# Another order of the 2,338 items of a twelve-stage decoder kernel

## The chip, the cores and the metric

One NeuronCore of one Trainium2 chip runs the whole program in a single launch. The metric is the device time of one execution in microseconds (us), the median of several runs. The chip's engines are called as in the profile: PE (TensorE matmuls), PEld (its weight loads), DVE (VectorE), ACT (ScalarE), POOL (GpSimd) and SP (SyncE, whose queue issues every DMA here, "SPq").

## The reference, cut to what is computed

The input `x` is (4, 512, 128): 4 batches of 512 tokens, model width 128. A context of 154 tokens per batch serves the cross attentions. Twelve stages follow each other, each as `x = layernorm(x + stage(x))`:

```python
CHAIN = ["L0a", "L0x", "ffn0", "heads1", "L1x", "moe1", "L2a", "L2x", "ffn2", "self3", "L3x", "moe3"]
# L0a, L2a: causal attention, 16 heads of width 8, rotated q and k
# L0x, L1x, L2x, L3x: cross attention to the context, 16 heads of width 8
# ffn0: quantised feed-forward with a depthwise convolution; heads1: attention among the heads of a token
# moe1: top 2 of 16 experts (with a capacity); moe3: 8 experts, dense; ffn2: gated feed-forward; self3: one-head attention
```

The 4 batches are independent, save for a running count of moe1's experts. So up to four chains of work can be interleaved.

## The kernel before

**Items.** The work is cut into items `(kind, stage and batch, number)`. `stage_items` (L150) lists them with what each needs. The six attention stages times 4 batches are the 24 *fronts*, numbered 0 to 23 in the order of `FRONT_ORDER` (0 to 3 are L0a, 4 to 7 L0x, 8 and 9 L1x, 10 L2a, 11 L1x, 12 L2a, 13 L1x, 14 and 15 L2x, 16 and 17 L2a, 18 and 19 L2x, 20 to 23 L3x). The other six stages are side stages. An item takes PE, and often DVE, ACT or POOL behind it, about 0.4 to 4 us.

**A front.** Its items come in this order:

- `project` (PE L782, L787): products for q, k, v. DVE copies them (L1244, L1248).
- `pieces` (POOL, `split_operands`, L1881): q, then k, are split into three bf16 pieces each, HQ and HK.
- `send` (SP, `load_operands`, L2000): the pieces are written to a DRAM scratch (L2010, L2014) and read back in another layout into QH and KH (L2025; L2032 and the `in_zrow` copy for a mask). Nothing of this takes PE.
- `max` (PE L824 and masks L830, then DVE L1261): scores q by k, of which DVE takes the negated row maxima. Two `max` items, one per half of the heads, make a step. A cross attention has 11 steps, a causal one 22. The first step of a front waits until its operands have landed (L801).
- `split`, `turn` (DVE, PE L840, ACT, DMA QH<-MT), then `pair` (PE L858, ACT's exponent L1683) and `value` (PE L897), `copy`, `out`, `mix`, and the tail `wo`, `square`, `mean`, `x`, which gives the stage's layernormed output to the next stage.

Side items that are named below: `gu` and `dn` are an expert's gate/up (PE L1017, L1018) and down product (PE L1024); `ew` is its weight load on SP's queue.

**What sets the order.** A list of words, `STEPS` (L257), says kind by kind which item comes next; a name with `*3` means three of it, and each `max` stands for a step of two. `ordered_items` (L337) takes the next waiting item of that kind, in the order of three short lists of stages and batches. `check_plan` (L455) asserts that every need stands ahead of its user. The result, PLAN, is walked once by each engine's program: every engine issues its own part of each item in this order, and waits in place for the semaphores that the item needs. The order is therefore the same on all engines, and an engine that waits for one item does none of the later ones. Products land in 3 single PSUM banks used in turn (`NRING` L606) and in two double ones for `pair`, `gu`, `g2`, `h0`, `s3`.

```python
                if F == 0:                                              # L797 to L801, PE ahead of a front's first max
                    pe.wait_ge(sem("fixed_rows"), 16 * 18)
                    ...
                pe.wait_ge(sem(f"operands_loaded{F % 3}"), operands_total(F))
```

Ahead of front 0's first max PE also waits for `halves_swapped` (L799): two copies CS<-const (`swap_halves`, L1984), which SP issues at the item `base`, once DVE has made `const` (DVE's part of `base`, L1169, its cast L1173). SP's part of `send` for front 0 is followed by `load_rest` (L1961): seven loads, among them pack<-in_pack of 2,284.5 KB.

Of the kernel before, what the change touches and what calls it, by code (L numbers as in the profile page):

```python
# [257 lines left out]
project*5 base pieces project send project*4 max*5 pieces max*9 send max*8 split project*2 max turn max project max pair  # L258
max project pair max pair max pair*2 max pair project value*3 pieces rest max pair*2 max pair max pair max value pair
max pair*2 max value max pair send pair max value max value pair max value copy pair*2 max value max project max value  # L260
max value pair max split pair project pair*2 max value turn pair max pair value max value*2 max pair*2 max value pair
copy max pair out pair out project max value max pair*2 max pair project max value max mix project pieces max value max
pair*2 max wo pair max value square pair max value max mean pair max value*2 max value pair copy max pair send x pair
max value max pair*2 value split out pair max pair turn pair*2 max value max value pair max pair value*2 max pair*2
value max pair value copy max pair*2 max value max pair*2 max value max project*2 out pair max value max pair*2 max
value max pair*2 masks value project mix project pieces pair*2 max value pair max value*2 pair max wo copy pair max
value send pair max pair value pair max pair value square max split pair*2 mean out x value turn value max pair project
value max pair*2 max value*2 pair max pair project*3 copy pair max pair value pieces max out value max pair*2 value max
pair mix pair max pair value*2 pair max value*2 pair max split pair wo send pair max value copy pair*2 max value max
pair square pair turn value max pair value max pair mean pair max value pair max value pair max value*2 max x pair value  # L270
pair max copy project out project pair max out project*2 pair value*2 pieces pair mix pair value pair send w0 copy split
wo turn out pair max value square pair max pair mean max value x max value project copy project out project*2 max mix
pair max wo max pair*2 max value square max mean max pair x pair max value pieces split send pair q0x pair value copy
pair*2 max q0t pair max h0 turn max h0 value*3 copy pair max silu0*3 out value silu0 out pair max h0t*2 mix pair h0b
pair max h0t wo h0b h0t square mean h0b*2 pair max x wo pair*2 q0x square value max pair*2 value q0t pair copy max h0
mean h0 value out silu0 value*2 silu0 copy max out silu0*2 h0t mix h0t h0b h0t h0b h0t h0b wo x h0b square wo max split
qkv mean qkv hs turn hv hs hm pair*2 qkv square value pair*2 hv value pair hs value hm qkv pair copy out pair mean
pair*2 tables2 pair value*2 hv hs hm value copy out mix x wo square mean hv hm x ht q0x wo q0t x square h0 mean x h0
# [1945 lines left out]
```

## Time and profile before

| what | us |
|---|---|
| median of 3 runs | 1750.06 |
| the 3 runs | 1750.06, 1750.02, 1759.99 |
| the profiled execution | 1757.96 |
| its span, first to last instruction | 1756.2 |
| PE busy in the span | 1378.9 |
| DVE busy | 1085.2 |
| ACT busy | 738.3 |
| POOL busy | 369.8 |
| mean granted clock of PE, share of 2.4 GHz | 0.866 |

The span and its 1.8 us of surroundings make the profiled execution's own time, which lies 7.9 us above the median, near the slowest of the three runs. An engine's busy time counts only what it computes; the rest of the span it waits, or issues. PEclk in a window is TensorE's granted clock as a share of 2.4 GHz: 0.50 is 1.2 GHz throughout.

### The profile page before, as it was taken

The page shows a single profiled execution, that of the slowest core. Times are in us where ns is not written, and L with a number is a line of the kernel's source. Part 1 is how long each engine was busy: PE and PEld are TensorE (multiplying, and loading weights), DVE is VectorE, ACT ScalarE, POOL GpSimd, SP SyncE. Part 2 cuts the span into 40 slices and gives each one's busy share as a digit, 9 for nine tenths or more (in the row PEclk, how much of TensorE's full clock was granted, in tenths as well). Part 3 has the DMA queues.
Part 4 walks back from the last instruction along what each step waited for, and adds up shares of the span by engine and source line. Part 5 has one row for each costly group of instructions (what it writes and reads, how often), then busy time and mean ns, then how long its engine had stood idle before and what let it go on. Part 6 is the DMA issues. An engine that isn't in the chain of part 4 may idle for free.

```text
span 1756.2 us, 25812 instructions
## 1 busy us (share of the span) xinstructions
PE 1378.9 (79%) x9530; PEld 656.8 (37%) x9530; DVE 1085.2 (62%) x2336; ACT 738.3 (42%) x1036; POOL 369.8 (21%) x475
## 2 busy tenths in 40 slices
PE   3568887785665686687577987988998999978986
PEld 1234332331331351343133544543344444434443
DVE  3648866778569579578766646756234524256766
ACT  1055654644323213214345542346644545532652
POOL 3034432006105206304432012022211100020000
PEclk8579988886567796798698989999999999988999
DMA  7421232100100310330222124131211321023011
GB/s 169 113 56 33 55 52 42 34 1 26 36 0 2 72 37 2 85 75 4 57 47 59 38 55 83 33 96 27 62 36 37 82 52 61 2 58 64 25 37 60
DMA packets 50072, 86.35 MB, mean 49 GB/s; under 512 B 13718, under 2 KB 42198, under 8 KB 45526
## 3 DMA queue, kind: packets, MB, share of 16 engines
q1 hardware_dynamic: 49950, 84.71, 21.0%
q8 instruction: 78, 1.28, 0.3%
q14 instruction: 44, 0.36, 0.1%
HBM read 66.95 MB, written 15.60 MB: 47 GB/s over the span
## 4 chain that ended last, share of the span: by engine, by line
PE 46%; DVE 18%; DMA 11%; POOL 7%; SPq 7%; issue 6%; ACT 5%; POOLq 0%; ACTq 0%; DVEq 0%
PE ps L897 5%; PE ps L1051 5%; PE ps L824 5%; DMA KH<-scratch 5%; DVE MX L1261 5%; PE ps L1017 4%; SPq L2025 4%; PE ps L1018 4%; PE ps L1024 3%; POOL SIDE L1937 3%; PE ps L830 3%; DMA scratch<-HQ 2%; PE ps L858 2%; PE ps L735 2%; ACT WORK L1683 2%
## 5 line engine op out<-in xcount | busy, mean ns | idle before, releaser
L1261 DVE TENSOR_REDUCE MX<-ps 128x3 f32<-128x462 f32 (+5 forms) x704 | 411.7, 626 | 233.4 <-PE ps L830 170.2
L1683 ACT ACTIVATE WORK<-ps 128x1024 f32<-128x1024 f32 (+1 forms) x352 | 319.7, 945 | 204.0 <-PE ps L858 123.9
L824 PE MATMUL ps<-KH,QH 48*128 48x154 bf16 (+5 forms) x1536 | 147.1, 279 | 178.0 <-DVE MX L1261 66.1
L824 PEld LDWEIGHTS ps<-KH,QH 48*128 48x128 bf16 (+1 forms) x1536 | 61.9, 99 | 334.7 <-DVE MX L1261 151.7
L897 PE MATMUL ps<-WORK,VA 128*18 128x512 f32 (+3 forms) x1536 | 171.4, 535 | 10.3 <-POOL WORK L1923 6.4
L1937 POOL TENSOR_TENSOR SIDE<-SIDE 128x512 f32<-128x512 f32 x64 | 113.1, 1799 | 269.1 <-ACT SIDE L1752 228.2
L1923 POOL TENSOR_SCALAR_AFFINE_SELECT WORK<-WORK 128x256 f32<-128x256 f32 (+1 forms) x192 | 93.8, 495 | 355.6 <-ACT WORK L1683 354.8
L1777 ACT ACTIVATE SIDE<-ps 128x512 f32<-128x512 f32 x96 | 57.3, 597 | 253.9 <-PE ps L1018 253.6
L858 PE MATMUL ps<-QH,KH 54*128 54x512 bf16 (+3 forms) x768 | 120.2, 359 | 13.8 <-ACT WORK L1683 10.8
L1507 DVE TENSOR_TENSOR SIDE<-SIDE,ps 128x512 f32<-128x512 f32 x96 | 65.6, 686 | 98.0 <-ACT SIDE L1777 97.5
L1024 PE MATMUL ps<-SIDE 128*128 128x128 f32 x768 | 111.0, 292 | 15.3 <-DVE SIDE L1507 13.0
L1017 PE MATMUL ps<-XT,SIDE 128*128 128x512 f32 x192 | 112.1, 668 | 6.8 <-DMA SIDE<-in_experts 6.7
L1024 PEld LDWEIGHTS ps<-SIDE 128*128 128x128 f32 x768 | 98.9, 200 | 42.9 <-issue 32.9
L1518 DVE SCALAR_TENSOR_TENSOR SIDE<-ps,SIDE 128x128 f32<-128x128 f32 x352 | 98.9, 343 | 18.6 <-PE ps L1024 16.7
L1018 PE MATMUL ps<-XT,SIDE 128*128 128x512 f32 x192 | 102.8, 618 | 0.0
L1876 POOL CAST HQ<-WORK 128x512 bf16<-128x512 f32 x23 | 14.2, 617 | 411.9 <-DVE WORK L1248 282.7
L858 PEld LDWEIGHTS ps<-QH,KH 54*128 54x128 bf16 x768 | 34.5, 99 | 100.8 <-issue 49.5
L946 PE MATMUL ps<-SQ,pack 128*128 128x512 f32 x96 | 61.1, 723 | 14.0 <-ACT SQ L1705 13.1
L735 PE MATMUL ps<-pack,SIDE 128*128 128x128 f32 x260 | 49.8, 337 | 28.2 <-DVE SIDE L1384 13.7
L782 PE MATMUL ps<-XT,pack 128*128 128x512 f32 x96 | 57.8, 711 | 14.2 <-DMA XT<-in_xT 10.1
L1626 ACT ACT_TABLE_LOAD x38 | 48.8, 1283 | 42.3 <-PE ps L858 13.3
L1316 DVE TENSOR_TENSOR XT<-YC,RS 128x512 f32<-128x512 f32 x48 | 36.2, 753 | 39.2 <-ACT RS L1715 39.1
(279 smaller groups left out, 2194.9 us busy)
## 6 DMA issues: line engine op xcount, KB each, us to landing
SIDE<-in_experts SPq DMA_DIRECT2D x96, 192.0 KB, 2.4
scratch<-HQ SPq DMA_DIRECT2D x48, 192.0 KB, 3.0
QH<-scratch SPq DMA_DIRECT2D x48, 192.0 KB
SIDE<-in_wide SPq DMA_DIRECT2D x8, 1024.0 KB, 6.6
QH<-scratch SPq DMA_DIRECT2D x48, 128.0 KB
scratch<-HK SPq DMA_DIRECT2D x16, 192.0 KB, 2.9
QH<-scratch SPq DMA_DIRECT2D x48, 64.0 KB
KH<-scratch SPq DMA_DIRECT2D x16, 192.0 KB
```

What stands on the lines that cost most here:

```text
L824: mms[b] = pe.matmul(banks[b][:, c * pitch:c * pitch + width], qr[b][:, h, t * 128:t * 128 + 128], kr[b][:, h, 0:width], start=(c == 0), s ...
L858: mm = pe.matmul(bank[:, b, q0 * (len(hs) == 1) + i * (S - q0):][:, 0:S - q0], kr[b][:, h, kt * 128:kt * 128 + 128], qr[b][:, h, q0:S], st ...
L897: mm = pe.matmul(ps[32 * j:32 * j + 2 * NV, UB, q0:S], lhsT.rearrange("p a c -> p (a c)"), PB[:, (PAIR_BASE[F] + where[pi]) % NSLOT, b, at ...
L1017: pe.matmul(banks[:, 0, :], gates(key, i)[:, 0:128], XT[:, b, :], start=True, stop=True)
L1018: pe.matmul(banks[:, 1, :], gates(key, i)[:, 128:256], XT[:, b, :], start=True, stop=True).then_inc(all_wide, 1)
L1024: mm = pe.matmul(bank[:, t * 128:t * 128 + 128], HID[n % 2][:, t * 128:t * 128 + 128], gates(key, i)[:, 256:384], start=True, stop=True, s ...
L1051: mm = pe.matmul(bank, hidden(l, k, c), src[:, k, :], start=(k == 0), stop=(k == FC - 1))
L1261: dve.tensor_reduce(MX[:, 32 * b + i0:32 * b + i0 + cnt], src, AX.X, ALU.max, negate=True).then_inc(freed, 1)
L1518: ins = dve.scalar_tensor_tensor(out=o, in0=p, scalar=s, in1=o, op0=ALU.mult, op1=ALU.add)
L1683: act.activation(PB[:, N % NSLOT, :, lo:hi], wide_banks("pair", F, n)[:, :, lo:hi], ACT.Exp).then_inc(sem("exp_done"), 1)
L1923: pool.affine_select(out=p, in_=p, pattern=pattern, compare_op=ALU.is_ge, fill=0.0, base=0, channel_multiplier=-1).then_inc(sem("selected" ...
L1937: pool.tensor_tensor(out[:, hs], SC1[i][:, hs].unsqueeze(2).broadcast_to([128, n_heads, DH, H]), v.broadcast_to([128, n_heads, DH, H]), AL ...
```

## The change

`STEPS` is replaced as a whole. Nothing else differs: the same 2,338 items, the same three lists of stages and batches, the same instructions, buffers and waits for each item. Two lines of the table, before and after (the others are of the same sort):

```diff
-project*5 base pieces project send project*4 max*5 pieces max*9 send max*8 split project*2 max turn max project max pair
+project*5 pieces project*5 send base max*2 pieces max*2 project max*4 project max*2 project max*3 project send max*2
```

Two places show what the words do. The first is the start of SP's queue, around front 0's `send` and the item `base` (CS<-const is `base`'s, scratch and QH/KH<-scratch are `send`'s, CT to mconst are `load_rest`). Before, in a piece of the difference:

```order
 L1982 DMA XT<-in_xT 128x1536
-L1988 DMA CS<-const 64x1088 x2
 L2010 DMA scratch<-HQ 64x3x512 x2
 L2014 DMA scratch<-HK 64x3x512 x2
```

and in the kernel after, further down:

```order
L2025 DMA KH<-scratch 8x4096 x2
L1963 DMA CT<-in_cT 128x640
L1964 DMA pack<-in_pack 128x4569
L1965 DMA SIDE<-in_mask_q 128x640
L1966 DMA SIDE<-in_mask_k 128x512
L1967 DMA SIDE<-in_mask_k 32x512
L1968 DMA SIDE<-in_mask_c 128x640
L1969 DMA mconst<-in_mconst 3x1
L1988 DMA CS<-const 64x1088 x2
L2010 DMA scratch<-HQ 64x3x512 x2
```

The two CS copies, which stood ahead of front 0's transfers, now stand behind them and behind the seven loads.

The second place is PE ahead of front 9's first max (L1x, batch 1; L779 is its last projection, L824 with 154 columns its first max step; L1017, L1018 and L1024 are experts of moe1, batch 0). Before:

```order
698 L779 MATMUL ps<-pack,CT 32x128 x4
699 L1017 MATMUL ps<-XT,SIDE 128x512
700 L1018 MATMUL ps<-XT,SIDE 128x512
701 L1024 MATMUL ps<-SIDE 128x128 x8
702 L1017 MATMUL ps<-XT,SIDE 128x512
703 L1018 MATMUL ps<-XT,SIDE 128x512
704 L824 MATMUL ps<-KH,QH 128x154 x6
```

After:

```order
704 L1024 MATMUL ps<-SIDE 128x128 x8
705 L1017 MATMUL ps<-XT,SIDE 128x512
706 L1018 MATMUL ps<-XT,SIDE 128x512
707 L1024 MATMUL ps<-SIDE 128x128 x4
708 L1017 MATMUL ps<-XT,SIDE 128x512
709 L1018 MATMUL ps<-XT,SIDE 128x512
710 L1017 MATMUL ps<-XT,SIDE 128x512
711 L1018 MATMUL ps<-XT,SIDE 128x512
712 L1024 MATMUL ps<-SIDE 128x128 x8
713 L1017 MATMUL ps<-XT,SIDE 128x512
714 L1018 MATMUL ps<-XT,SIDE 128x512
715 L824 MATMUL ps<-KH,QH 128x154 x6
```

Between the last projection and the first max step PE has two `gu` and two `dn` (four products each) before, and four `gu` and five `dn` after. Counted from the k projection, which stands earlier, it is 4 `gu` and 4 `dn` before and 6 `gu` and 5 `dn` after.

## Rows read from the trace of the kernel before

**Rows 1.** The page: span, busy time by engine, chain by engine
```profile
span 1756.2 us, 25812 instructions
...
PE 1378.9 (79%) x9530; PEld 656.8 (37%) x9530; DVE 1085.2 (62%) x2336; ACT 738.3 (42%) x1036; POOL 369.8 (21%) x475
...
PE 46%; DVE 18%; DMA 11%; POOL 7%; SPq 7%; issue 6%; ACT 5%; POOLq 0%; ACTq 0%; DVEq 0%
```

**Rows 2.** Waits of PE: line waited for: us, times, longest
```profile
PE ps L824 <- DVE MX L1261: 66.1, 100, 4.8
PE ps L824 <- DMA KH<-scratch: 62.6, 12, 11.5
PE ps L824 <- DMA KH<-in_zrow: 20.4, 3, 8.7
PE ps L824 <- DMA KH<-MK: 17.3, 3, 7.4
```

**Rows 3.** Timeline, front 15: start us, us, engine line op [idle before]
```profile
1023.30 0.61 POOL L1876 CAST HQ<-WORK 128x512 bf16<-128x512 f32 x1 [46.82 <-DVE WORK L1248]
...
1028.47 0.49 POOL L1879 TENSOR_TENSOR HK<-WORK,HK 128x160 bf16<-128x160 f32 x1
...
1028.99 1.24 SPq L2014 DMA_DIRECT2D scratch<-HK  x2
...
1032.98 2.25 SPq L2025 DMA_DIRECT2D KH<-scratch  x6
...
1041.93 0.57 PE L824 MATMUL ps<-KH,QH 48*128 48x154 bf16 x6 [6.53 <-DMA KH<-scratch]
```

**Rows 4.** Windows, k projection to first max, of fronts 6, 7, 9, 15
```profile
core 0: us, PE busy (x) PEld busy (x) DVE busy (x) ACT busy (x) POOL busy (x), PEclk, DMA share, GB/s
...
271.70:291.00 19.30, 10.75 (x79) 4.16 (x78) 11.44 (x35) 8.40 (x11) 5.15 (x8) 0.89 0.47 84
300.80:319.40 18.60, 12.57 (x122) 4.59 (x122) 14.87 (x39) 11.54 (x15) 5.13 (x8) 0.95 0.45 85
...
592.80:614.40 21.60, 11.97 (x58) 6.98 (x58) 8.67 (x27) 2.57 (x5) 6.74 (x11) 0.92 0.60 118
...
1022.50:1041.90 19.40, 11.72 (x77) 4.82 (x76) 5.93 (x15) 8.80 (x12) 5.14 (x8) 0.89 0.60 111
```

**Rows 5.** Groups by line, whole span
```profile
L1017 PE MATMUL ps<-XT,SIDE 128*128 128x512 f32 x192 | 112.1, 668 | 6.8 <-DMA SIDE<-in_experts 6.7
L1024 PE MATMUL ps<-SIDE 128*128 128x128 f32 x768 | 111.0, 292 | 15.3 <-DVE SIDE L1507 13.0 <-DVE SIDE L1518 1.1 <-DVE MX L1261 0.5
L1018 PE MATMUL ps<-XT,SIDE 128*128 128x512 f32 x192 | 102.8, 618 | 0.0
```

**Rows 6.** Timeline of SP's queue, 24 to 58 us
```profile
24.61 1.18 SPq L1988 DMA_DIRECT2D CS<-const  x2
...
36.50 0.44 SPq L1964 DMA_DIRECT2D pack<-in_pack  x1
...
39.63 1.24 SPq L2010 DMA_DIRECT2D scratch<-HQ  x2
...
54.89 2.30 SPq L2025 DMA_DIRECT2D QH<-scratch  x6
```

**Rows 7.** Windows, first to last max, fronts 0, 8, 9; sum of 24
```profile
47.40:83.50 36.10, 19.39 (x193) 10.79 (x193) 24.91 (x42) 0.00 (x0) 0.00 (x0) 0.50 0.46 118
...
478.90:527.50 48.60, 33.18 (x130) 16.54 (x130) 31.65 (x72) 11.40 (x17) 0.00 (x0) 0.66 0.00 0
614.40:656.10 41.70, 37.18 (x196) 21.95 (x196) 30.29 (x75) 5.97 (x10) 0.00 (x0) 0.92 0.14 39
...
sum 974.20, PE 836.03 PEld 413.22 DVE 670.63 ACT 420.50 POOL 185.20; mean PE 34.83 PEld 17.22 DVE 27.94 ACT 17.52 POOL 7.72
```

**Rows 8.** Windows behind five waits: the first (front 9), the sum
```profile
614.40:621.20 6.80, 6.79 (x25) 4.02 (x26) 3.40 (x8) 0.00 (x0) 0.00 (x0) 0.50 0.09 29
...
sum 37.30, PE 35.51 PEld 19.41 DVE 20.89 ACT 7.21 POOL 0.00; mean PE 7.10 PEld 3.88 DVE 4.18 ACT 1.44 POOL 0.00
```

More of the change, by code:

```diff
@@ L257 @@
 STEPS = """
-project*5 base pieces project send project*4 max*5 pieces max*9 send max*8 split project*2 max turn max project max pair
[L259 to L277, printed above, removed]
@@ new lines @@
+value qkv value hm copy pair*2 hs pair hv hm value hv qkv pair mean hs value out hm pair x value hv copy out mix wo hm
+square x mean ht q0x wo q0t x square h0 mean x h0 project silu0*4 project h0t*2 h0b h0t h0b h0t h0b project*2 h0b pieces
+send wo max q0x max*2 q0t max*2 h0 max h0 square silu0 max silu0*3 max h0t*2 h0b h0t h0b h0t h0b max h0b max wo max qkv
+mean split qkv hs turn pair*2 hv pair hs hm qkv hv pair*3 value hs value hm square hv qkv value pair*3 copy value*2 pair
+value hs hm out mean copy out x hv mix wo hm square mean x*2 ht log top ew*2 wo gu square ew rank gu mean dn x dn ew gu
@@ new lines @@
+ew project gu dn*2 project ew project gu*2 project dn pieces dn ew*2 gu dn ew send gu*2 ew dn*2 ew gu ew max gu max dn*2
+ew max gu max gu dn*2 ew max ew gu max dn max ew gu max gu max dn*2 max acc max split qkv*2 hs wo square turn hv hs pair
+qkv pair*2 hm hv value*2 pair*2 mean qkv value pair hs pair copy x pair hm pair hv project pair hs value hm project
+value*2 project copy out*2 mix project wo hv project square mean hm x ht log top ew wo gu pieces square ew*2 rank gu
+mean dn send ew dn x ew gu project*2 gu max dn project ew dn max ew gu max gu dn ew max dn max gu max ew gu max dn*2 max
@@ new lines @@
+square pair max mean max value x max project max pair project max*2 pair max out pair max project*2 max mix out max
+pieces value max pair wo square max value max copy send mean split out turn mix x max wo project square pair*2 max mean
+pair max x pair value max pair log pair max pair value project ew max top pair ew pair value pair value project*2 pieces
+pair*2 max value pair max ew pair value pair max gu*2 rank value*2 copy max pair value dn send pair*2 out ew dn pair*2
+max value*2 split pair*2 max ew gu*2 turn max pair value pair dn value ew max pair dn gu*2 ew value max pair dn*2 ew
@@ new lines @@
+pair max gu ew gu value*2 max copy pair dn out dn gu max ew value*2 mix dn gu ew gu max pair dn wo pair dn ew max ew
+pair square pair ew value pair max pair mean max x gu copy project gu dn value dn gu ew project split value*2 ew dn turn
+gu*2 copy dn out dn project pair*2 acc out wo project mix value square pieces send wo mean square max pair x mean max
+pair*2 x max pair log project top max ew*2 gu value rank project gu dn project*2 dn ew*2 gu ew gu dn project ew dn max
+gu*2 dn max value dn pieces ew*3 gu copy max send pair*2 max dn gu max gu dn pair max pair max split dn ew gu ew value
@@ new lines @@
+hid2 max pair*2 max wo max pair value max pair*2 max pair value max value max wide copy pair*2 value max pair value max
+out g2*2 square value copy max g2 max g2 wide out mean x split hid2 mix hid2*3 wo hid2*2 turn square hid2*2 pair*2 wo
+pair*2 f3 mean s3 square x s3 fk3 value pt3*4 mean x wo value f3 square mean s3 x s3 project pair project fk3 pt3*4 pair
+wo square value copy log project ew project pair top ew*2 pair out mean gu*2 pieces send max dn*2 x max gu ew max
+project*2 dn max gu max pair value ew max dn pair max ew gu project max gu value project max value pieces send max ew
@@ L329 @@
+ew gu*2 dn ew dn gu ew dn gu square gu dn*2 fin mean acc wo square x mean x fin*2
 """.split()
```

95 lines of the change are left out of this document (44 added, 51 removed).

## The prediction

> **What bounds the kernel now.** I read the page first. PE is busy 1378.9 of 1756.2 us, DVE 1085.2; no engine is full, and the chain that ended last runs 11% over DMAs and 7% over SP's queue [rows 1]. So look for where PE stands still for a transfer. PE's waits say it: 66.1 us in 100 small waits for DVE's maxima, and 100.3 us (62.6 + 20.4 + 17.3) in only 18 waits at L824 for KH [rows 2]. L824 is the score product of a `max` item, and KH is what `send` fetches, so these 18 are waits of a front's first max step.
>
> The timeline of front 15 shows one of them whole [rows 3]. Its k projection ends at 1022.5, POOL splits q and k from 1023.3 to 1029.0, the scratch writes and the read-back are issued up to 1035.2, and PE starts at 1041.9, after 6.5 us of nothing. Set against that the work that PE had in the meantime: in the 19.4 us from the k projection to the first max it was busy 11.7 [rows 4]. Fronts 6, 7 and 9 read the same: 19.3, 18.6 and 21.6 us, filled with 10.8, 12.6 and 12.0 us [rows 4]. The latency of a cross front is thus about 19 us, that of a rotated causal one some 5 us more (POOL's longer split), and the order before puts too little work between.
>
> **The change, step by step.** The same instructions run, so I price places only.
>
> *1. Waits for the first max.* For each front I added up PE's time for the items between its last q/k projection and its first max, in both orders, each item at the time that its own instructions took in the trace. Front 9 as the example: 4 `gu` and 4 `dn` before, 6 and 5 after. A `gu` is (112.1 + 102.8)/96 = 2.24 us, a `dn` 111.0/96 = 1.16 [rows 5], so 2 x 2.24 + 1.16 = 5.6 us more. But SP's queue counts too: front 9's `send` stands behind an `ew` that waits for a `dn`, and from that `dn` to the first max the work grows only by 4.1 us. Of its wait (7.4 us, the longest of the MK row [rows 2]) 3.3 are left. In the same way: fronts 4, 5, 6 and 7 gain 2.6, 7.4, 8.4 and 10.2 us of cover against waits of 1.1, 4.7, 3.1 and 3.7, so nothing is left; 8, 17 and 19 gain 5 to 7 against 4.8, 6.3 and 4.5, nothing left; 10, 12, 13, 15 and 16 keep 2.1, 2.2, 1.8, 0.7 and 0.3; front 14 keeps 4.6 (its cover is counted from the last causal select ahead of `pieces` on POOL); front 18 gains none and keeps 1.8; front 22 gains 3.9 against 11.5 and keeps 7.6. The 89 us of these fronts (100.3 less front 0's 10.9, from 36.5 to 47.4) fall to 25, a gain of 64. Some of the moved items were timed at the low clock and will be shorter, so I take 58. Bounds: 79 if every one goes that gains cover at all, 45 if the items shrink by a third.
>
> *2. Front 0 starts later.* `base` now stands behind `send` on SP. Before, SP issued the two CS copies at 24.6 [rows 6], and PE started at 47.4 on its operands. Now they are issued behind `load_rest`, at about 39.6, where the next write stood, and PE waits for them. What a transfer issued there meets is in the trace: the query write of front 1, issued at 39.63 behind the 2,284.5 KB of pack (36.50), was not there for SP's next step until 54.89 [rows 6]. So the CS copies land near 55 and PE starts some 8 us later: +8. Bounds: 0, if small copies get past the load, and 12. The page "DMA: Bandwidth & Descriptors" of the Trainium skill, in its section on latency, names about 2 us as the fixed cost of a DMA; priced by that alone the copies would be there at 42, ahead of the operands, and the sum would be 8 us lower. The same page's section on queues says that each DMA engine takes descriptors in ring order, which is what the row shows.
>
> *3. Cover taken out of the max phases.* The work now ahead of the first max was elsewhere: mostly inside other max phases, where it ran while DVE reduced. Over the 24 phases PE is busy 836 us and DVE 671 in 974 [rows 7]; by the same item times the new order leaves PE 783 there, 53 us less. What bare steps look like is seen in front 0, with nothing between: 36.1 us for 24.9 of DVE and 19.4 of PE, 22 steps of 1.64 us [rows 7], in which both engines wait for each other by turns. I cut both orders into short stretches (3 to 30 items) and took the busier engine's time in each: the new order is longer by 1 to 7 us in sum. That is the low bound, since it knows no latencies. The high bound is that all 53 us stop being hidden. I take 14, near the low end, as most phases still have PE above DVE.
>
> *4. The clock.* Behind a long wait PE runs at half speed. After the waits of fronts 9, 10, 15, 16 and 17 the granted clock is 0.50 for 37.3 us in all, with PE busy 35.5 of them [rows 8]; at the full level that is half the time, 18 us. The other waits have such stretches too, but in phases where DVE also binds. I take -18, bounds 0 and -30.
>
> *5. Other distances* (turn to pair, log to rank, value to out, heads1's chain) I compared the same way: some shrink and some grow by 1 to 6 us, in sum about nothing. The loads of the experts and of ffn2 keep their places relative to their users within a few items.
>
> Sum: -58 + 8 + 14 - 18 = -54. Against the profiled execution's own 1757.96 that is 1704. It lies 7.9 above the median, and since the runs before show both 1750.0 and 1760.0 I take half of that off: **1700 us**. A measurement here tells about 1% (17 us) from no change.
>
> **The rivals.**
>
> *A. The max phases lose what the fronts gain.* One mechanism: the 53 us moved out of the phases were fully hidden there and now cost their full length, and the thinner phases fall to the low clock, so the 18 us do not come. For it: front 8's phase, where PE (33.2) only matches DVE (31.7), took 48.6 us at a clock of 0.66, and front 0's ran at 0.50 throughout [rows 7]. Against it: front 9's phase, with PE above DVE, lost only 4.5 us to gaps [rows 7]. Price: -58 + 8 + 53 + 0, and some 15 us more for phases 1, 8 and 9 at half clock: +18, so 1776, and **1772** as a median. It decides from 50 us of lost cover on. The Trainium skill has the rule in "TensorE: Matmul & The Clock Gate", in the section on a second failure mode (depth-cycling of PSUM): short idles between groups of matmuls, often enough, make the clock oscillate. Front 0's phase agrees ((36.1 - 19.4)/22 = 0.76 us without PE in each step, clock 0.50).
>
> *B. Half of it.* The waits go, but what fills them runs faster than in the trace and what is late next (DVE's maxima, the exponent) takes half of the gain: -27, so 1731, **1728** as a median. For it: PE's waits for DVE's maxima are many and short, 66.1 us in 100 [rows 2], and the new order makes more of them. Against: late in the kernel PE is near full in most windows.
>
> *C. The change does not do what it says.* SP issues in order, so a `send` that stands behind an `ew` or a `turn` starts only when these may; if the landings move back with the max steps, the 18 waits stay and front 0's +8 is all: **1755**. For it: front 9, above. Against: for the other fronts the item ahead of `send` on SP's queue is ready before the split is done, in both orders.
>
> **How the numbers follow.** Forecast 0.75, B 0.11, A 0.07, C 0.07. The forecast's own range comes from its bounds, not all at one end at once: 1663 to 1728. Faster by over 1% (below 1732.6) is nearly all of the forecast's share and over half of B's: 0.81. Within 1%: C, the rest of B and a little of the forecast: 0.13. Slower by over 1%: most of A: 0.06. The range 1664 to 1742 leaves out A and C, some 0.14, and a little at the low end.
>
> **What would show it.** Right, if PE's waits for KH fall from 100 us to 30 to 45 in all, the longest two being front 0's (near 19 us) and front 22's (7 to 8); if PE's first max starts near 55 instead of 47.4; if the mean granted clock rises above 0.866; if DVE's maxima are waited for somewhat more than 66 us. Wrong in term 1, if fronts 5 to 8 and 15 to 17 still wait over 2 us each. Wrong in term 2, if the first max stays at 47. Wrong in term 3 (rival A), if the waits for KH are gone and the 24 max phases with less PE work are not shorter.

## The result and the profile after

The changed kernel takes 1689.2 us (median of 4 runs, 1681.2 to 1693.0) beside 1752.8 for the kernel before (the three runs above and a fourth, 1755.6): a ratio of 0.963, 95% interval [0.960, 0.966]. Four single executions among all the runs below, of 2,221 to 6,492 us and two of them of e4_max_late, were slow ones and are left out of every time and ratio. Forecast were 1700 us and 1664 to 1742. The profiled execution took 1692.3 us, 65.7 less than the one of before; the forecast worked out from it was 54 less.

The page of the kernel after: span, busy time by engine, granted clock in 40 slices, chain by engine (of before [rows 1]).

```profile
span 1690.6 us, 25807 instructions
...
PE 1359.3 (80%) x9530; PEld 648.6 (38%) x9530; DVE 1084.9 (64%) x2336; ACT 736.6 (44%) x1035; POOL 372.9 (22%) x475
...
PEclk8559899987666797799779999999999999989989
...
PE 54%; DVE 20%; DMA 7%; ACT 6%; issue 5%; POOL 4%; SPq 4%; ACTq 0%; DVEq 0%; POOLq 0%
```

DVE, ACT and POOL are busy as long as before. PE is busy 19.6 us less on the same products, because less of them falls at 1.2 GHz: summed from the clock records of the two traces, PE is busy 311.8 us at that level before and 267.4 after (mean clock 0.866 and 0.882; an estimate of the same work at the full level, with half of that time taken off, is 1223 us before and 1226 after). It stands still 46.0 us less (span less busy time: 377.3 before, 331.3 after). On the chain DMA fell from 11 to 7% and SP's queue from 7 to 4%.

PE's waits after: line waited for, us in total, times, longest (of before [rows 2]).

```profile
PE ps L824 <- DVE MX L1261: 63.2, 83, 4.0
PE ps L871 <- DMA QH<-MT: 21.1, 5, 9.6
PE ps L1017 <- DMA SIDE<-in_experts: 19.8, 5, 7.5
PE ps L858 <- ACT WORK L1683: 17.9, 18, 4.4
PE ps L824 <- DMA CS<-const: 17.9, 1, 17.9
PE ps L897 <- ACT WORK L1683: 16.9, 5, 8.8
...
PE ps L824 <- DMA KH<-scratch: 13.1, 4, 8.3
```

The 100.3 us for KH are 13.5 (13.1 here, 0.4 in another row), with front 22's the longest. Front 0 now waits 17.9 us for CS instead of 10.9 for KH. The wait for MX is not longer than before. New are three long waits for an expert's load.

The windows of the max phases of fronts 0, 8 and 9 and the sum of all 24 (of before [rows 7]); columns: us; busy time of PE, PEld, DVE, ACT, POOL; PEclk; DMA share; GB/s.

```profile
57.00:99.10 42.10, 29.02 (x209) 14.24 (x209) 27.64 (x46) 0.63 (x1) 9.57 (x10) 0.50 0.22 42
...
482.00:524.10 42.10, 25.71 (x121) 13.81 (x120) 31.03 (x71) 8.69 (x14) 0.00 (x0) 0.68 0.00 0
623.10:652.60 29.50, 24.25 (x149) 13.70 (x148) 23.97 (x57) 4.18 (x7) 0.00 (x0) 0.96 0.09 27
...
sum 913.50, PE 779.19 PEld 384.15 DVE 668.17 ACT 422.59 POOL 190.76; mean PE 32.47 PEld 16.01 DVE 27.84 ACT 17.61 POOL 7.95
```

The phases lost 56.8 us of PE's work and got 60.7 us shorter: PE stands still in them 134.3 us, against 138.2 before. Outside the phases the kernel takes as long as before (777 us, 782 before), with 37 us more of PE's work in it.

SP's queue from 36 to 60 us, where the CS copies now stand (of before [rows 6]).

```profile
36.39 0.43 SPq L1964 DMA_DIRECT2D pack<-in_pack  x1
...
39.31 1.16 SPq L1988 DMA_DIRECT2D CS<-const  x2
40.74 1.28 SPq L2010 DMA_DIRECT2D scratch<-HQ  x2
45.89 5.77 SPq L2014 DMA_DIRECT2D scratch<-HK  x2
57.64 2.28 SPq L2025 DMA_DIRECT2D QH<-scratch  x6
```

The copies are issued 2.9 us behind `pack`, and PE starts its first max 17.7 us after their issue, at 57.0. Before it was 47.4. The view of DMA issues from 24 to 62 us gives the time from issue to landing (last figure, median of the two copies), before and then after:

```profile
CS<-const SPq DMA_DIRECT2D x2, 136.0 KB, 5.1
```

```profile
CS<-const SPq DMA_DIRECT2D x2, 136.0 KB, 16.5
```

### The profile page after: what moved, and what is told of

It reads as the page before. It is cut to its first block, busy times and chain, and to the rows that moved or that the text cites. A ratio compares the mean times of both kernels' runs of the same rounds, so it can differ in the third digit from the quotient of the medians.

```text
span 1690.6 us, 25807 instructions
## 1 busy us (share of the span) xinstructions
PE 1359.3 (80%) x9530; PEld 648.6 (38%) x9530; DVE 1084.9 (64%) x2336; ACT 736.6 (44%) x1035; POOL 372.9 (22%) x475
## 4 chain that ended last, share of the span: by engine, by line
PE 54%; DVE 20%; DMA 7%; ACT 6%; issue 5%; POOL 4%; SPq 4%; ACTq 0%; DVEq 0%; POOLq 0%
PE ps L897 6%; PE ps L1051 6%; PE ps L824 6%; DVE MX L1261 5%; PE ps L1017 5%; PE ps L1024 4%; PE ps L1018 4%; POOL SIDE L1937 3%; PE ps L830 3%; PE ps L735 3%; PE ps L782 3%; PE ps L858 2%; DMA SIDE<-in_experts 2%; SPq L2025 2%; ACT WORK L1683 2%
## 5 line engine op out<-in xcount | busy, mean ns | idle before, releaser
L824 PE MATMUL ps<-KH,QH 48*128 48x154 bf16 (+5 forms) x1536 | 142.4, 271 | 104.5 <-DVE MX L1261 63.2
L897 PE MATMUL ps<-WORK,VA 128*18 128x512 f32 (+3 forms) x1536 | 165.7, 518 | 20.8 <-ACT WORK L1683 14.9
L824 PEld LDWEIGHTS ps<-KH,QH 48*128 48x128 bf16 (+1 forms) x1536 | 59.1, 96 | 268.2 <-DVE MX L1261 156.2
L858 PE MATMUL ps<-QH,KH 54*128 54x512 bf16 (+3 forms) x768 | 118.0, 352 | 19.8 <-ACT WORK L1683 17.9
L1017 PE MATMUL ps<-XT,SIDE 128*128 128x512 f32 x192 | 112.1, 668 | 20.1 <-DMA SIDE<-in_experts 19.8
L1024 PE MATMUL ps<-SIDE 128*128 128x128 f32 x768 | 110.1, 290 | 18.4 <-DVE SIDE L1507 14.9
L1024 PEld LDWEIGHTS ps<-SIDE 128*128 128x128 f32 x768 | 97.6, 198 | 49.4 <-issue 36.2
L1518 DVE SCALAR_TENSOR_TENSOR SIDE<-ps,SIDE 128x128 f32<-128x128 f32 x352 | 98.8, 343 | 18.5 <-PE ps L1024 16.5
L1018 PE MATMUL ps<-XT,SIDE 128*128 128x512 f32 x192 | 102.5, 616 | 0.0
L782 PE MATMUL ps<-XT,pack 128*128 128x512 f32 x96 | 66.0, 796 | 23.2 <-DMA XT<-in_xT 14.5
L858 PEld LDWEIGHTS ps<-QH,KH 54*128 54x128 bf16 x768 | 33.7, 97 | 98.4 <-ACT WORK L1683 54.7
L1626 ACT ACT_TABLE_LOAD x38 | 48.8, 1283 | 30.2 <-PE ps L858 7.6
L946 PE MATMUL ps<-SQ,pack 128*128 128x512 f32 x96 | 55.1, 657 | 7.7 <-ACT SQ L1705 7.3
L897 PEld LDWEIGHTS ps<-WORK,VA 128*18 128x18 f32 x1536 | 30.2, 98 | 75.8 <-issue 29.2
```

What stands on the lines that cost most here:

```text
L782: mm = pe.matmul(bank[:, 0:src.shape[1]], w, src, start=True, stop=True)
L824: mms[b] = pe.matmul(banks[b][:, c * pitch:c * pitch + width], qr[b][:, h, t * 128:t * 128 + 128], kr[b][:, h, 0:width], start=(c == 0), s ...
L858: mm = pe.matmul(bank[:, b, q0 * (len(hs) == 1) + i * (S - q0):][:, 0:S - q0], kr[b][:, h, kt * 128:kt * 128 + 128], qr[b][:, h, q0:S], st ...
L897: mm = pe.matmul(ps[32 * j:32 * j + 2 * NV, UB, q0:S], lhsT.rearrange("p a c -> p (a c)"), PB[:, (PAIR_BASE[F] + where[pi]) % NSLOT, b, at ...
L1017: pe.matmul(banks[:, 0, :], gates(key, i)[:, 0:128], XT[:, b, :], start=True, stop=True)
L1018: pe.matmul(banks[:, 1, :], gates(key, i)[:, 128:256], XT[:, b, :], start=True, stop=True).then_inc(all_wide, 1)
```

## The experiments

Each is a new `STEPS`, with the same items and instructions, so nothing is left out of the computation. A cover is PE's work, in us of the trace, between a front's last q/k projection and its first max. The table puts all of them side by side. They ran in four groups, in each of which the kernel before was timed too (medians 1752.3, 1750.5 and 1750.0, and 1747.9 for the last; 1.000 and the 1750.1 of the table are the three runs above); between groups the ratios compare better than the times. Time and ratio are of the timed runs, the rest of the one profiled execution: PE busy (the page), PE still (span less busy), and PE's waits in groups, each summed from the rows of the view of PE's waits. "KH, CS" are the first max steps, "MX" is L824 waiting for maxima, "turn" is L840's wait for MP and every wait for QH<-MT (split, turn, first pair), "experts" is L1017's for in_experts. The five groups add up to 10 to 13 us less than "PE still": that rest no row of the view names.

| kernel | time | ratio to before, 95% | PE busy | PE still | KH, CS | MX | turn | experts | all other |
|---|---|---|---|---|---|---|---|---|---|
| before | 1750.1 | 1 | 1378.9 | 377.3 | 100.3 | 66.1 | 24.0 | 6.7 | 170.0 |
| e0_after | 1687.0 | 0.965 [0.962, 0.969] | 1353.1 | 331.0 | 30.3 | 64.9 | 24.5 | 17.6 | 180.9 |
| e1_base_first | 1678.2 | 0.958 [0.954, 0.962] | 1356.0 | 323.8 | 23.8 | 64.7 | 25.6 | 21.5 | 175.6 |
| e7_best | 1678.5 | 0.959 [0.957, 0.961] | 1358.3 | 316.6 | 22.1 | 70.0 | 23.7 | 6.3 | 182.4 |
| e5_ew_first | 1699.2 | 0.971 [0.968, 0.975] | 1360.5 | 334.7 | 51.9 | 64.2 | 24.0 | 3.5 | 178.4 |
| e3_send_late | 1711.1 | 0.977 [0.973, 0.980] | 1359.5 | 349.7 | 34.3 | 64.8 | 20.9 | 35.5 | 181.5 |
| e6_bare17 | 1715.5 | 0.980 [0.978, 0.982] | 1368.8 | 339.8 | 30.9 | 80.0 | 22.5 | 19.4 | 175.1 |
| e8_max_early | 1751.8 | 1.001 [0.998, 1.004] | 1384.0 | 370.3 | 83.5 | 70.2 | 19.7 | 3.2 | 181.7 |
| e2_base_late | 1759.3 | 1.004 [1.001, 1.007] | 1381.1 | 381.7 | 101.5 | 65.0 | 24.7 | 6.2 | 173.5 |
| e10_max_late9 | 1758.4 | 1.003 [1.001, 1.006] | 1376.1 | 384.1 | 68.2 | 87.1 | 34.4 | 5.3 | 179.5 |
| e11_shift | 1754.0 | 1.003 [1.001, 1.005] | 1375.0 | 370.5 | 30.5 | 72.2 | 51.5 | 20.6 | 185.0 |
| e4_max_late | 1762.2 | 1.008 [1.005, 1.011] | 1387.6 | 371.3 | 30.2 | 91.9 | 33.7 | 24.5 | 181.1 |
| e9_late_even | 1788.6 | 1.020 [1.014, 1.026] | 1394.7 | 393.5 | 32.6 | 90.2 | 33.4 | 17.7 | 208.3 |

**e0_after**: the changed kernel as it is.

> The changed kernel again, as the mark for the others that are made from it. Expected 1689 us (0.963 of the kernel before, as measured), and in its trace the same pattern as in the first: PE's wait for CS<-const near 18 us, for KH some 13 us, for the expert loads (SIDE<-in_experts) some 20 us. A theory that puts one of these down to chance would see it change here.

The pattern repeats: CS 17.6, KH 12.7, experts 17.6. PE's busy time was 6.2 us less than in the first profile of the same kernel (254.0 us of it at 1.2 GHz, 267.4 there), so differences of that size between two profiles prove nothing.

**e1_base_first** and **e2_base_late**: the price of `base` behind `load_rest`, from both sides.

```diff
 e1_base_first, against the changed kernel
-project*5 pieces project*5 send base max*2 pieces max*2
+project*5 base pieces project*5 send max*2 pieces max*2
 e2_base_late, against the kernel before
-project*5 base pieces project send project*4 max*5
+project*5 pieces project send project*4 base max*5
```

> The changed kernel with `base` ahead of front 0's pieces and send, as it stood before. Theory (the two CS copies are late only because they are issued behind load_rest): the first max starts at 47.5 us again instead of 57.0, PE's wait for CS<-const (17.9 us) is replaced by one of some 11 us for KH, and the time falls by 8 to 10 us against the changed kernel. Rival (the start is paid back later, since front 1's items are not ready sooner): the first max starts 9 us earlier but the phase of front 0 or the wait for front 1 grows by as much, and the time stays within 3 us.

> The kernel before with `base` moved to directly ahead of front 0's first max, so that its CS copies stand behind load_rest as in the changed kernel, and nothing else. Theory: the first max starts at 55 to 57 us instead of 47.4 and the whole kernel gets 8 to 10 us slower. Rival (the delay is absorbed later, as front 1 waits for DMAs anyway): 0 to 3 us slower.

PE's first max in e1_base_first, then in e2_base_late, from the timelines (start, us, what; in brackets the idle time before and what ended it):

```profile
48.03 0.61 PE L824 MATMUL ps<-KH,QH 48*128 48x512 bf16 x2 [11.34 <-DMA KH<-scratch]
```

```profile
57.39 0.61 PE L824 MATMUL ps<-KH,QH 48*128 48x512 bf16 x2 [17.53 <-DMA CS<-const]
```

The one item moves the start by 8 to 10 us in both kernels, and the wait changes its name with it. In the changed kernel undoing it is worth 8.8 us (1687.0 to 1678.2), as expected. In the kernel before it costs 7 us (0.4%, interval 2 to 12 us), which decides neither for the 8 to 10 expected nor against the rival's 3. Its trace shows something of both: the first max of a front stands 9 to 14 us later than before up to front 15 and 5 to 7 us later from front 16 on, so part of the delay is taken up by waits on the way (the KH waits of fronts 5, 14, 15 and 16 are each 1.3 to 1.8 us shorter).

The copies themselves land 5.5 us after their issue in e1_base_first and 16.4 us in e2_base_late, by the same view as above. In either kernel it is some 5 us when they are issued ahead of the load and some 16 behind it.

**e5_ew_first**: three loads of experts (not four, as its expectation says) ahead of the sends. One of the three edits, at front 9:

```diff
-ew*2 gu dn ew send gu*2 ew dn*2 ew gu ew max
+ew*2 gu dn ew*2 send gu*2 dn*2 ew gu ew max
```

> The changed kernel with four loads of experts issued ahead of a front's send instead of behind it: those of moe1 batch 0 expert 9 (ahead of front 9's send), batch 1 expert 3 (front 10's), batch 3 expert 9 (front 16's, with the down product whose space it reuses). Theory (an expert's load waits behind the read-backs on SP's in-order queue): PE's waits for SIDE<-in_experts, 19.8 us in three places, fall to 2 us or less, and the time falls by 10 to 18 us. Rival (the queue only passes the delay on: the sends now wait for the loads): the first max of fronts 9, 10 and 16 waits 2 to 6 us each instead, and the time stays within 4 us.

The expert waits fall to 3.5 us (to 2 or less was expected), and the kernel gets 12 us slower: the rival's mechanism, and worse than its price. SP's queue around front 10's `send` in the changed kernel (e0_after), then here:

```profile
708.80 1.28 SPq L2051 DMA_DIRECT2D SIDE<-in_experts  x3
710.19 1.29 SPq L2010 DMA_DIRECT2D scratch<-HQ  x2
```

```profile
709.59 12.53 SPq L2051 DMA_DIRECT2D SIDE<-in_experts  x4
722.23 1.29 SPq L2010 DMA_DIRECT2D scratch<-HQ  x2
...
728.50 2.25 SPq L2025 DMA_DIRECT2D KH<-scratch  x6
```

The group of loads stretches over 12.5 us instead of 1.3. Expert 3 goes into the space of expert 0, so its load waits for expert 0's down product, and the `send` behind it waits too: it starts 12 us later. Front 10's first max then waits 12.9 us instead of 0, front 9's 6.8, front 16's 3.4.

**e3_send_late**: meant to place `pieces` and `send` later. It did not do so, and its expectation describes it wrongly.

```diff
-ew wo gu pieces square ew*2 rank gu mean dn send ew dn x ew gu project*2 gu max
+ew wo gu pieces send square ew*2 rank gu mean dn ew dn x ew gu project*2 gu max
```

> The changed kernel with `pieces` and `send` of thirteen fronts (4 to 10, 12, 13, 15, 16, 17, 19) placed later, so that PE has as much work between the split and the first max as in the kernel before (within about 2 us); PE's own order stays that of the changed kernel. Theory (this distance is what the change wins by): the waits for KH of these fronts come back, 68 us in the kernel before, with the low clock behind them: 60 to 85 us slower than the changed kernel, that is 1745 to 1770. Rival (the gain lies in the rest of the order, and the waits went because everything ahead of them moved): under 25 us slower.

I had set the work between `send` and first max to what stands between projection and first max in the kernel before. In the changed kernel `send` stands nearer to the first max than that in twelve of the thirteen fronts, so there it moved earlier, as the edit at front 10 shows; only front 5's moved later (19.6 us of PE's work behind it, now 14.1). So this run says nothing for or against the distance. It says two other things. Front 5, the one that moved later, waits 3.9 us for KH instead of 0. And where a `send` moved ahead of expert loads (fronts 9, 10 and 16), the loads wait behind it. SP's queue at front 10, then PE behind it:

```profile
717.97 1.28 SPq L2010 DMA_DIRECT2D scratch<-HQ  x2
...
726.15 2.25 SPq L2025 DMA_DIRECT2D KH<-scratch  x6
728.45 0.83 SPq L2051 DMA_DIRECT2D SIDE<-in_experts  x2
```

```profile
738.07 2.05 PE L1017 MATMUL ps<-XT,SIDE 128*128 128x512 f32 x2 [11.95 <-DMA SIDE<-in_experts]
```

PE could have had expert 1 at 726.1; its load is issued at 728.45, behind twelve read-back pieces, and PE starts at 738.1. Three such waits (11.95, 10.4 and 10.0 us) make most of the 35.5 of the table. The kernel lost 20 to 24 us by ratio and times; between the traces it is 25.1, of which 18.7 are PE standing still. Together with e5: neither place of an expert's load beside a `send` is free.

**e8_max_early**: the distance taken out of the changed kernel (front 9 here).

```diff
-ew send gu*2 ew dn*2 ew gu ew max gu max dn*2
+ew send max gu*2 max ew dn*2 max ew gu ew gu dn*2
```

> The reverse of e4_max_late on the changed kernel: the first 1 to 4 max steps of thirteen fronts (4 to 10, 12, 13, 15, 16, 17, 19) are drawn forward, so that 56 us of PE's work leave the stretches between the q/k projections and the first max and stand in the max phases again. e3_send_late did not do this: POOL and SP run ahead of PE, so a later place in PE's list did not delay a split or a send. Theory (distance on PE between projection and first max is worth its waits): waits of 35 to 50 us for KH come back in fronts 5, 7, 8, 9, 10, 19, and with the low clock behind them the kernel gets 35 to 60 us slower than the changed kernel (1722 to 1747). Rival (what e4_max_late showed: cover in front of the first max and cover inside the phases are worth the same): KH waits come back, but MX and expert waits fall by nearly as much, under 15 us slower.

(Its sentence on e3_send_late is wrong, as said above.) The whole gain is gone: 1751.8 us, as the kernel before and 62 to 65 us above the changed one (by the ratios, by the times), more than the expected 35 to 60. Between the two profiles, 70 us apart, 39.3 us are PE standing still and 30.9 are PE busy longer on the same work, at a clock of 0.861 instead of 0.886 (busy at 1.2 GHz for 322.4 us instead of 254.0). PE's waits at L824 here:

```profile
PE ps L824 <- DVE MX L1261: 70.2, 78, 4.5
PE ps L824 <- DMA KH<-scratch: 38.8, 10, 7.8
...
PE ps L824 <- DMA CS<-const: 17.6, 1, 17.6
PE ps L824 <- DMA KH<-MK: 16.2, 3, 10.0
```

KH came back with 53 us. The work that went back into the phases saved nothing there: MX is 70.2 against 64.9, and PE's idle time in the 24 phases 148 us against 138. Only the expert waits fell, from 17.6 to 3.2, since PE comes later to the gate/up products. The rival is out: in the changed kernel the whole gain hangs on where the first steps of these thirteen phases stand.

**e4_max_late**: the same distance given to the kernel before (front 9 here).

```diff
-gu pieces dn*2 send ew gu max dn max ew gu ew gu dn*2 max gu ew gu
+gu pieces dn*2 send ew gu dn ew gu ew gu max dn max dn max gu ew gu
```

> The kernel before with nothing changed but the place of the first 1 to 6 max steps of fourteen fronts (4 to 10, 12, 13, 15, 16, 17, 19, 22): they are postponed behind the work that followed them until PE has as much ahead of the first max as in the changed kernel. Theory (the cover ahead of the first max is worth its waits, and the max phases lose little by it): these fronts' 80 us of waits fall to 15 to 25, the mean clock rises to 0.875 or more, the time falls by 50 to 75 us. Rival A (the phases lose what the fronts gain): the waits fall as much, but PE's waits for MX and its idle time inside the 24 phases grow by 50 us, and the time falls by less than 15 us.

The waits for KH fall by 70 us (without front 0 from 89.4 to 20.0; the changed kernel has 12.7), and the time does not fall: it is 0.8% longer than before (13 us; 2.7 between the profiled executions, of which the one of before was among the slower of its kernel). In the time this is what rival A forecast, in the trace only a part of it: summed over the 24 phases, from the first L824 of each to its last, PE's idle time grew from 137.8 to 158.6 us, where the expectation has 50 more, so most of what came back stands outside the phases. Four of the rows that moved:

```profile
PE ps L824 <- DVE MX L1261: 91.9, 128, 5.2
PE ps L1017 <- DMA SIDE<-in_experts: 24.5, 6, 9.8
PE ps L824 <- DMA KH<-scratch: 22.4, 5, 10.2
...
PE ps L858 <- DMA QH<-MT: 8.3, 3, 6.6
```

Against the kernel before, MX costs 26 us more, experts 18, turned maxima 10, the rest 11: 64 of 70 are back. And PE is busy 8.7 us longer, at 0.865, with 325.8 us of it at 1.2 GHz against 311.8 before: the long waits went and the clock did not rise. That splits what the prediction had tied together: the absence of the KH waits does not bring the clock's gain by itself. Three of the new expert waits show where a part of it went: behind each, PE's first products run at 1.2 GHz, as they did behind the KH waits (L1017 takes 2.04 us for two there, and 1.10 at 716.6 us, behind a wait of 0.5).

**e10_max_late9**: e4 in only the nine fronts without a moe1 load right behind their send (front 5 here).

```diff
-max value copy pair*2 max value max pair square pair turn value max pair value max pair mean pair
+value copy pair*2 value pair square pair turn value pair value pair mean max pair max*2 value max
```

> e4_max_late with only the nine fronts whose send has no load of a moe1 expert right behind it (4, 5, 6, 7, 8, 12, 17, 19, 22): 42 us of KH waits in the kernel before. If e4_max_late lost because the waits at fronts 9, 10, 13, 15, 16 only moved to the gate/up products (SIDE<-in_experts 24.5 us there against 6.7), this one keeps the gain of its own nine: expert waits near 7, KH waits near 65, time 15 to 25 us below before. If the phases lose what the fronts gain, the time stays within 8 us of the kernel before.

The expert waits stay away (5.3 us) and the gain too: KH falls by 32 us, MX rises by 21, the turned maxima by 10, all other by 10. So the experts alone were not what e4 lost by. MX carries most of it:

```profile
PE ps L824 <- DVE MX L1261: 87.1, 125, 5.2
```

**e9_late_even**: e4 with its steps spread evenly by PE's time (front 17 here).

```diff
-max pair max*2 value max*2 pair max value max*2 value pair max out pair*2
+max pair value max pair value max value max pair max out pair max pair value
```

> e4_max_late with the steps of its fourteen fronts spread evenly over the phase by PE's time, the first and the last step and all other items in place. Steps with nothing between them and the one before fall from 31 to 22 in these phases. If e4_max_late lost by bunching (a step without cover waits for DVE's maxima, and PE falls to the low clock), PE's waits for MX fall from 92 us to 75 or less, the clock rises and the time falls to 1740 or less. If the cover missing in the phases as a whole is what costs, it stays within 8 us of e4_max_late's 1765.

MX is 90.2, no better, and the kernel 21 us slower still (by the ratios). An even spread by PE's time did not help: front 8's phase alone grew from 44.6 to 55.0 us, and the all-other column by 27. That bunching is the cause was not shown here, nor excluded, since 22 bare steps (with no work of PE between them and the step before) remained in these phases, by the expectation's count.

**e11_shift**: the phases of e4 begun later and ended later, with few steps left bare (front 9 here).

```diff
-gu pieces dn*2 send ew gu max dn max ew gu ew gu dn*2 max gu ew gu
+gu pieces dn*2 send ew gu dn ew gu ew gu dn*2 max gu ew gu dn ew dn ew*2 max gu max gu
```

> The kernel before with the max phases of the same fourteen fronts (4 to 10, 12, 13, 15, 16, 17, 19, 22) begun 1 to 6 steps later, as in e4_max_late, but not made up for inside the phase: every step takes the place of a later one, the last ones stand behind the old end of the phase, one after each 0.6 us or more of PE's work, and split and turn follow them. PE's cover ahead of the first max is that of the changed kernel (within 3 us). Max steps with no PE work between them and the one before number 40 over all 24 phases in the kernel before, 32 in the changed one, 58 in e4_max_late, 34 here. Theory (the cover pays only if no step is left bare): KH waits near 31 us as in e4_max_late, MX waits back from 92 to 75 us or less, the clock above 0.87, and the time 30 to 60 us below the kernel before, 1690 to 1720. Rival (the phases' later end costs what their later start gains: split, turn and the first pair come later): MX waits fall as said, but PE waits 20 us or more longer for turned maxima, exponents and expert loads, and the time is within 10 us of the kernel before.

MX falls back to 72.2 us, as the theory said, which fits e4's rise of MX having come from the bare steps. The time does not follow (1754.0; the profiled execution lies 10.7 us below the one of before, the timed runs 0.3% above). The rival's sentence holds: what was paid at MX is now paid at turn and pair.

```profile
PE ps L824 <- DVE MX L1261: 72.2, 111, 5.4
PE ps L824 <- DMA KH<-scratch: 20.7, 4, 10.2
PE ps L1017 <- DMA SIDE<-in_experts: 20.6, 6, 8.2
PE ps L871 <- DMA QH<-MT: 19.7, 9, 8.9
PE ps L840 <- DVE MP L1276: 17.8, 9, 4.5
PE ps L858 <- DMA QH<-MT: 14.0, 5, 7.1
```

The last three rows are split, turn and first pair: 51.5 us, 24.0 before. One of them in the timeline of PE, front 16:

```profile
1172.06 1.05 PE L897 MATMUL ps<-WORK,VR 128*18 128x512 f32 x8
1180.26 0.61 PE L858 MATMUL ps<-QH,KH 54*128 54x512 bf16 x2 [7.15 <-DMA QH<-MT]
```

The phase ends later and its items are used up, so nothing is left to cover the way of the maxima through DVE, PE, ACT and a DMA into QH.

**e6_bare17**: one phase stripped.

```diff
-max pair value out pair max copy pair*2 max value max pair*2 out wide
+max*22 pair value out pair copy pair*2 value pair*2 out wide
```

> The changed kernel with one max phase stripped: the items that stand between the 22 steps of front 17 (27.4 us of PE's time in the trace) come behind the phase's last step but one. It measures the price of lost cover. In the changed kernel the phase takes 40.1 us, PE busy 38.1 and DVE 27.8. If all the moved work was hidden and now costs its length, the bare phase takes 36 us as front 0's did in the kernel before, at the low clock, and the kernel gets 27.4 + 36 - 40 = 23 us slower. If the phase only falls back to what DVE needs (25 us, at a clock kept high), it gets 12 us slower. If the moved items run faster elsewhere, less than 8 us.

Slower by 1.5% of the ratios, 26 us, and by 24.6 in the profiles. The windows of front 17's phase and of the stretch behind it, in the changed kernel (e0_after), then here:

```profile
1139.30:1179.40 40.10, 38.10 (x428) 16.75 (x427) 27.85 (x52) 29.43 (x36) 11.51 (x24) 1.00 0.08 27
```

```profile
1135.20:1170.10 34.90, 18.10 (x195) 10.44 (x194) 24.91 (x42) 0.69 (x1) 0.00 (x0) 0.58 0.08 30
1170.10:1205.00 34.90, 31.77 (x235) 10.04 (x232) 5.40 (x16) 28.10 (x34) 11.55 (x24) 0.88 0.00 1
```

The first line is the changed kernel, the second and third are this one. The bare phase takes 34.9 us with PE busy 18.1 at a clock of 0.58, much like front 0's bare phase before (36.1 us at 0.50) [rows 7]: without cover PE and DVE take turns. The 27.4 us taken out shorten the phase by 5.2 only, so cover in the middle of a phase is worth most of its length, in one phase at least. The first theory (23 us) was right.

**e7_best**: e1 with four more moves (front 22 here).

```diff
-gu*2 pieces send max dn*2 x max gu ew max project*2 dn
+gu*2 pieces send dn*2 x gu ew project*2 dn gu max*2
```

> A version meant to beat both: the changed kernel with `base` ahead of front 0's send (as in the run that tried it alone, 1678), the first max of front 22 behind 25.7 instead of 17.4 us of PE's work (four steps postponed) and of front 18 behind 21.6 instead of 17.9, and two gate/up items that waited for their expert's load (moe1 batch 1 expert 3, batch 3 expert 9) placed one to three items later. Expected: the KH waits of fronts 22 (7.5) and 18 (1.7) gone, the two waits for experts (2.8 and 5.8) down to 2 in all, so 12 to 15 us less than with `base` alone: 1664 to 1668. If the phases of 18 and 22 lose as much or the loads are then late at the next item, 1675 to 1680.

Both aims were met: front 22's first max waits for nothing, as its row in PE's timeline shows by naming no wait, and the expert waits are 6.3 us.

```profile
1501.91 0.37 PE L824 MATMUL ps<-KH,QH 48*128 48x154 bf16 x6
```

Yet the time is that of e1_base_first, 1678.5 beside 1678.2, though the profile shows 5 us less: MX took 5 us and the all-other column 7, and fronts 10, 16 and 15 wait 3.4, 3.3 and 3.2 us at their first max instead (front 15 waited 1.5 in e1_base_first). The sentence for the failing case (1675 to 1680) holds. e1 and e7 are the two versions that beat both kernels, by some 9 us or 0.5% against the changed one; which of the two is the faster can't be told.

## Why the prediction was right, and where it was not

The time was right (1689 in 1664 to 1742), and the mechanism that carried it was the one predicted: e8_max_early takes it out and loses everything. But the number is closer than its terms are: terms 1 and 3 were off by 18 and 14 us to one side, term 5 by 20 to the other, and that they cancelled is luck. Between the two profiles, as measured: fronts 1 to 23 at their first max -75.9, front 0 there +7.0, all other waits +20.5 (those inside the phases among them), standing still that no row names +2.4, PE's busy time -19.6: -65.6.

*Term 1, waits for the first max: -58 predicted.* Fronts 1 to 23 fell from 89.4 to 13.5 us, -76, inside the bounds of 45 to 79. Fronts 5 to 8, 16 and 17 wait for nothing and 15 for 1.3, as predicted. Fronts 22 (8.3; predicted 7.6), 18 (2.8; 1.8), 19 (0.7; nothing) and 12 (0.4; 2.2) keep something; 9, 10, 13 and 14 keep nothing, where 3.3, 2.1, 1.8 and 4.6 were predicted. For fronts 9 and 10 a reason is in the trace: PE waits 5.1 and 5.2 us just before them for an expert's load, and what it waits there it does not wait at the first max. Front 16, which came out as predicted, has the same behind it: 7.5 us for an expert's load up to 1064.9, and its first max at 1069.5. These three waits make 17.8 us, and with them set against it the term is -58, the number predicted. So the cover was right, and the sum over fronts missed that a wait can move to the item ahead of the first max. The same exchange is in e8 (KH up 53, experts down 14).

*Term 2, front 0 starts later: +8.* Shown: the start moved by 9.6 us. The wait is 17.9 us (near 19 was predicted), 7.0 more than before, and PE's wait for its input at the very start is 4.4 longer (14.5 us at L782 for in_xT, 10.1 before). `base` alone is worth 8.8 us in the changed kernel and some 7 in the one before.

*Term 3, cover taken out of the phases: +14.* Measured about nothing: PE's idle time in the phases went from 138.2 to 134.3, and MX, which was to rise somewhat, fell from 66.1 to 63.2. The step that failed was the low bound's: it held that thinner phases must cost at least a little. In the changed order they don't. Counted from the two orders, 27 steps have no item of PE between them and the step before, against 37 before (e11_shift's expectation, by a count of its own, has 32 and 40), although 57 us less of such work stand in the phases: it is spread better over them. That is a reading of the orders and not a proof. e11_shift supports it (32 such steps and an MX of 72 us, against 50 and 92 in e4), but the count is not all: e8_max_early has the same 27, with more cover in the phases, and its MX is 70.2.

*Term 4, the clock: -18.* PE's busy time fell by 19.6 us in the first profile and 25.8 in the second. The size was right, though part of it is the execution that was profiled: it read a clock of 0.866, and the executions of the kernel before read 0.863 to 0.880, 0.871 on average. The reason was too narrow. I had tied it to the low clock behind the KH waits. In e4_max_late those waits are gone and PE is busy 8.7 us longer. Over all the runs PE is busy longer where it stands still more, but only roughly: in the table 1353 to 1361 us of work go with 317 to 350 us of standing, 1375 to 1395 with 370 to 394. Taken run by run it does not hold: e6_bare17 stands still 10 us less than e3_send_late and is busy 9 longer, and e10_max_late9 stands 13 us more than e4_max_late and is busy 11 less. What moves with the busy time is how much of it falls at 1.2 GHz (254 us in e0_after, 270 in e3, 285 in e6, 303 in e10, 326 in e4). Which waits cause that no run separates.

*Term 5, other distances: about nothing.* This was the worst of the five. All waits but those for KH and CS grew from 266.8 to 287.3 us, +20.5. Experts are 13.1 of it, the exponents (L858 and L897 on WORK) 17.2, turned maxima 5.0 (QH<-MT), and others fell. The failing sentence was that the experts' loads "keep their places relative to their users within a few items". They did, within six; but on SP's queue three had moved up to the first place behind a `send` (from the fourth, second and third), and on PE their gate/up products had come to stand ahead of that front's first max instead of behind it. SP, then PE at expert 9 of moe1, batch 3, in the kernel after:

```profile
1049.97 2.25 SPq L2025 DMA_DIRECT2D KH<-scratch  x6
1052.26 0.61 SPq L2036 DMA_DIRECT2D KH<-in_zrow  x2
1052.91 1.05 SPq L2051 DMA_DIRECT2D SIDE<-in_experts  x2
```

```profile
1064.93 2.04 PE L1017 MATMUL ps<-XT,SIDE 128*128 128x512 f32 x2 [7.49 <-DMA SIDE<-in_experts]
```

The prediction read SP's queue for front 0 and front 9 and not for the loads behind the sends. For the exponents' 17.2 us no run shows the cause.

*The rivals.* C is out (its 1755 does not follow from its own words either: +8 on the profiled execution is 1766, 1762 as a median). B's mechanism did come, at a smaller price: waits of the kind it names took 20.5 of the 68.9 us back and not half, by the exponent, as it said, and the experts, but not by DVE's maxima. A had 7% and did not come in this change, yet its outcome is real: the same distance, given to the kernel before in three ways (e4, e10, e11), gained nothing. The waits move on to MX, to turn and pair, to the experts. So the distance is needed for the gain (e8) but does not bring it alone. An item-by-item sum, as in term 1, can't see where a wait moves: it would have given e4 its 50 to 75 us as well, and did, in its expectation. What in the rest of the changed order keeps those other waits at +20 us instead of +63 stays open. The bare steps are probably part of it (e11 against e4: MX 20 us less) but not all, and no run here adds the missing part to the kernel before. One reading that stood for A was too loose: front 0's phase shows a granted clock of 0.50 throughout, so its short idles go with a low clock, not with one that swings between the two levels.

## What to carry to other kernels

Work that fills a wait for a transfer may be missed where it stood: moving it cost nothing in the changed kernel and the whole gain in three other orders. Before counting such a gain, name what each moved item covered before, and look at the step that comes out of the other end of the phase (here split, turn and first pair), since postponing a start postpones that too. In a kernel whose every engine walks one list, an item's place matters against its neighbours on its own queue: list them for SP, above all bulk loads that carry a wait of their own, and read from each run both PE's idle time and its busy time, as in these runs both moved. An edit that is meant to move something later should be shown to do so, from the order itself, before its run is believed.

## What the runs showed of the hardware

- Two CS copies of 136 KB issued at 39.3 us, 2.9 us behind a bulk load of 2,284.5 KB, took 16.5 us from issue to landing, and PE started 17.7 us after their issue. Issued ahead of the load they took 5.1 to 5.5 us (before, e1_base_first). Copies that small were not passed ahead of the load. Two writes of HK behind it stretch over 5.77 us on SP's queue, where they take 1.24 for front 15 [rows 3]; the copies are not the reason, as these writes stretch over 5.36 us in the kernel before too.
- A bare phase kept TensorE low even in the second half of the kernel (e6_bare17): granted clock 0.58 with PE busy 18.1 of 34.9 us, where the covered phase had 1.00 with 38.1 of 40.1, and 0.88 in the 34.9 us behind it, with PE busy 31.8 of them.
- Removing 70 us of long waits did not raise the clock (0.865 in e4_max_late, 0.866 before; 0.867 and 0.871 on average over the executions of that group) while others took their place; 39 us more of standing still in e8_max_early came with 31 us more of busy time on the same products.
